# Two moves in the instruction order of a tuned fp32 kernel: GpSimd's w3 product ahead of its edge steps, ScalarE's square root one iteration later

## The chip, the cores and the metric

The kernel runs on one core of a Trainium2 chip. The metric is the device time of one execution, in microseconds, from the first to the last instruction of the program with what little lies around them. Five engines share the work: TensorE (PE in the profile; its weight loads are PEld), VectorE (DVE), ScalarE (ACT), GpSimd (POOL) and SyncE (SP), which only issues the DMAs here. Each engine runs its instructions in the order in which they were written for it. An engine that waits for a semaphore holds up all that stands behind it on its own queue.

## What is computed

Four blocks, one after the other, each add to x a chain of four style-modulated 1D convolutions over 64 samples of 64 channels and 1024 positions, in fp32:

```python
def _layer(x, style, w, b, mw, mb, typ):
    s = style @ mw.T + mb
    weight = SCALE * w * s[:, None, :, None]
    demod = lax.rsqrt(jnp.sum(weight * weight, axis=(2, 3)) + EPS)
    weight = weight * demod[:, :, None, None]
    if typ == 'same':
        out = conv_same(x, weight) + b[None, :, None]
    elif typ == 'upsample':
        out = blur(conv_up(x, weight) + b[None, :, None])
    elif typ == 'downsample':
        out = conv_down(blur(x), weight) + b[None, :, None]
    return out
# in each of four blocks, with the block's own weights:
for typ in ('same', 'upsample', 'same', 'downsample'):
    out = _layer(out, style, ...)
x = x + out
```

The weights differ from sample to sample, since the style scales them. Layers 1 to 3 of a block have nothing nonlinear between them, so for each sample the kernel folds them into one short filter.

## The kernel before

**The main loop.** It has NN = 256 iterations, one for each pair of block and sample: 4 blocks of 64 samples, the block number being k. n is the iteration, and n mod 64 the place within a block. For each sample TensorE runs `conv0` (layer 0, 6 matmuls of 512 columns, into the bank `ZP`) and `convg` (the folded filter, 12 matmuls). Every fp32 operand is held as a high and a low part, so a product is three matmuls. TensorE's iteration n issues `conv0(n + 1)`, what edge and setup work falls due, and then `convg(n)`.

**What lies between the two convolutions.** ScalarE writes the high part zh from PSUM (`zhi`, L721), VectorE then the low part zl (`zlo`, L980), and `convg` waits for zl. Ahead of `conv0` stand in the same manner xh (`xhi`, L709, ScalarE) and xl (`xlo`, L974, VectorE). After `convg` VectorE adds the result into the resident X (`xnew`, L989), and SyncE stores it.

**The folded filters.** They are made for four samples at a time (QS = 4), in a chain across the engines. GpSimd multiplies w3 by the samples' scales into w3q (`w3s`, L1279), at n = 3 mod 4. ScalarE rounds it to w3h (`w3hi`, L735) at the head of its iteration n = 0 mod 4. GpSimd makes the low parts of it (`w3lo`, L1285 and L1286). TensorE multiplies by w2 (`v_products`, output of L1010 on VectorE), then by w1 (`k_products`, weights w1h, w1l, w1d). ScalarE evicts the result to kp in eight instructions (`kev`, L750), four on either side of `zhi`, and VectorE makes the filter taps out of kp (L1031 to L1043) and their low part (L1067).

**GpSimd's iteration.** In written order it holds: in the last block `finish`, which corrects the edges of a finished sample; a gather of edge columns; `edge_apply` (L1402 to L1405); one of the four edge steps (z, y, s, o) of the block; `w3lo`; `w3s`; and tables that are built at a few iterations. The edge steps fall at n mod 64 = 4, 7, 9 and 11, in the first block at 16, 19, 21 and 23. Step y (L1369 to L1375) waits for VectorE's yq and step o (L1388) for VectorE's en. Both stand in an iteration that also has a `w3s`.

**Setup of the next block.** During a block its scales for the next one are made in stages at fixed iterations: VectorE's reciprocal and ScalarE's square root (stage RECIP) at n = 27 in the first block and at n mod 64 = 15 in the next two, VectorE's Newton step (NEWTON, L892) four iterations on. ScalarE's square root (`root`, L684) waits for VectorE's reciprocal (L883), the last work of VectorE's iteration, and stands last in ScalarE's iteration.

The functions and what calls them follow.

Of the kernel before, what the change touches and what calls it, by code (L numbers as in the profile page):

```python
# [40 lines left out]
SQUARES, STYLE, DEMOD, NEWTON, TABLES, BIAS_U, BIAS_S, SPLIT_W, SPLIT_1, RECIP = range(10)  # L41
# [47 lines left out]
def build(nc, x, ends, pack, taps, w3in, small, sets, out):  # L89
    ctx = ExitStack()  # L90
    with ctx:
# [115 lines left out]
        def where(n):  # L207

            st, i = divmod(n, GS)
            g, k = STEPS[st]  # L210
            return st, k, g * GS + i, n % (NR * GS)
# [9 lines left out]
        def v_at(n):  # L221
            if n in V_LATE or n in V_LATE.values():
                return (V_LATE[n] + V_LEAD) // QS if n in V_LATE else None
            q, i = divmod(n + V_LEAD, QS)
            return q if i == 0 and 0 <= q < NQ else None

        def g_at(n):
            if n in G_LATE or n in G_LATE.values():
                return (G_LATE[n] + G_LEAD) // QS if n in G_LATE else None
            q, i = divmod(n + G_LEAD, QS)  # L230
            return q if i == 0 and 0 <= q < NQ else None
# [27 lines left out]
        def finished_at(n):  # L259

            first = (NBLK - 1) * NB
            start = first + EDGE_SLOT + EDGE_STEPS[-1] + 1
            done, at = [], first
            for i in range(start, n + 1):
                done = list(range(at, min(at + 4, i - 1, NN)))
                at += len(done)
            return done
# [9 lines left out]
        def setup_at(n):  # L277
            k, i = n // NB + 1, n % NB
            if k == NBLK - 1 and i == LAST_BIAS_S:
                return k, (BIAS_S,)  # L280
            return (k, (SECOND_SLOTS if k == 1 else SETUP_SLOTS).get(i, ())) if k < NBLK else (None, ())
# [364 lines left out]
        def _(act):  # L646
# [4 lines left out]
            def squares(k):  # L651
                act.activation(wsq[:, 0:3], wT[:, k], ACT.Square)
                act.activation(wsq[:, 3], w1T[0:C, k], ACT.Square).then_inc(s["wsq"], 1)

            def w2hi(k):
                if k >= NW:
                    act.wait_ge(s["V"], (k - NW + 1) * NB // QS)
                act.activation(w2h[:, k % NW], w2f[:, k], ACT.Copy)
                act.activation(w2d[0:C, k % NW, 0:K], w2f[0:C, k, 0:K], ACT.Copy)
                act.activation(w2d[C:128, k % NW], w2f[0:C, k], ACT.Copy).then_inc(s["w2hi"], 1)  # L660

            def w0hi(k):
                if k >= NW:
                    act.wait_ge(s["conv0"], (k - NW + 1) * NB)
                act.activation(w0h[:, k % NW], w0f[:, k], ACT.Copy).then_inc(s["w0hi"], 1)

            def w1hi(k):
                if k >= NW:
                    act.wait_ge(s["K"], (k - NW + 1) * NB // QS)
                act.activation(w1h[0:C, k % NW, 0:K], w1T[0:C, k], ACT.Copy)  # L670
                act.activation(w1h[C:128, k % NW, 1:K + 1], w1T[C:128, k], ACT.Copy)
                act.activation(w1d[:, k % NW, 0:K], w1T[:, k], ACT.Copy).then_inc(s["w1hi"], 1)
# [9 lines left out]
            def root(l, count):  # L682
                act.wait_ge(s["rcp"], count)
                act.activation(dall[:, l, :], tmp[:, l, :], ACT.Sqrt).then_inc(s["sqrt"], 1)  # L684

            def setup(k, stage):
                if stage == SQUARES:
                    act.wait_ge(s_pack[k], 16)
                    act.wait_ge(s_taps[k], 16)
                    act.wait_ge(s["Dp"], k)  # L690
                    squares(k)
                    w2hi(k)
                    w0hi(k)
                elif stage == RECIP:
                    root(slice(0, NLAY), k + NPART)
                elif stage == SPLIT_W:
                    w1hi(k)

            def xhi(n):
                st, k, b, sl = where(n)  # L700
                act.wait_ge(s["S0"], k + 1)
                if k == 0:
                    p, use = pair_of(n)
                    act.wait_ge(s_in[p], 16 * use)
                else:
                    act.wait_ge(s["eap"], applied(st))
                if n >= 3:
                    act.wait_ge(s["conv0"], n - 2)
                act.activation(xh[n % 3][:, 0:XW], X[:, sl, :], ACT.Copy, scale=tab["S0"][:, k, b:b + 1]) \  # L709
                    .then_inc(s["xhi"], 1)  # L710
# [20 lines left out]
            def w3hi(q):  # L731
                act.wait_ge(s["w3q"], q + 1)
                if q >= 1:
                    act.wait_ge(s["V"], q)
                act.activation(w3h[:, :, :, :], w3q[:, :, :, :], ACT.Copy).then_inc(s["w3h"], 1)  # L735

            def vhi(q):
                act.wait_ge(s["vf"], q + 1)
                if q >= 1:
                    act.wait_ge(s["K"], q)  # L740
                act.activation(vh[:, 0:2, :, :], vf[:, 0:2, :, :], ACT.Copy).then_inc(s["vh"], 1)
                act.activation(vh[0:C, 2, :, :], vf[0:C, 2, :, :], ACT.Copy).then_inc(s["vh2"], 1)
# [9 lines left out]
            def kev(q, part):  # L752
                if part == 0:
                    act.wait_ge(s["K"], q + 1)
                    act.wait_ge(s["t1s"], STEPS[q * QS // GS][1] + 1)
                    act.wait_ge(s["fir"], q)
                for j in range(QS):
                    ins = evict(q, j, part)
                if part == 1:
                    ins.then_inc(s["kev"], 1)  # L760
# [82 lines left out]
            for n in range(2, NN):  # L843
                if v_at(n + 1) is not None and n + 1 not in V_LATE:
                    w3hi(v_at(n + 1))
                if n + 3 < NN:
                    xhi(n + 3)
                if g_at(n) is not None:
                    kev(g_at(n), 0)
                if n + 1 < NN:  # L850
                    zhi(n + 1)
                if g_at(n) is not None:
                    kev(g_at(n), 1)
                if g_at(n - 2) is not None:
                    ghi(g_at(n - 2))
                if v_at(n - 1) is not None:
                    vhi(v_at(n - 1))
                k, stages = setup_at(n)
                for stage in stages:
                    setup(k, stage)  # L860
                if where(n)[1] == NBLK - 1:
                    xb(n)

# [359 lines left out]
        def _(pool):  # L1223
            counts, open_ = {"w3q": 1, "w3l": 1}, {}

            def sig(ins, name="chp", by=1):

                ins.then_inc(s[name], by)
                counts[name] = open_[name] = counts.get(name, 0) + by
# [41 lines left out]
            def w3s(q):  # L1271
                st, k, b, sl = where(q * QS)
                if k >= 1:
                    pool.wait_ge(s["e2"], k)
                    pool.wait_ge(s["w3rest"], 16)
                pool.wait_ge(s["w3l"], q)
                e = tab["E2"][:, k, b:b + QS].unsqueeze(1).unsqueeze(3).broadcast_to([128, 2, QS, C])
                w = w3f[:, k, :, :].unsqueeze(2).broadcast_to([128, 2, QS, C])
                sig(pool.tensor_tensor(w3q[:, :, :, :], w, e, ALU.mult), "w3q")  # L1279
# [144 lines left out]
            pool.wait_ge(s["xlo"], 4)  # L1424
            for n in range(NN):
                st, i = divmod(n, GS)
                for m in finished_at(n):
                    finish(m)
                if i == GATHER and st >= 1 and STEPS[st - 1][1] < NBLK - 1:
                    gather(st - 1)  # L1430
                if ends_at(n) is not None:
                    ends_ready(ends_at(n))
                if i == APPLY and st + 1 < NS and STEPS[st + 1][1] >= 1:
                    edge_apply(st + 1)
                k, stage = edge_at(n)
                if k is not None:
                    (edge_z, edge_y, edge_s, edge_o)[stage](k)
                if v_at(n + 1) is not None:
                    w3lo(v_at(n + 1))
                if v_at(n + 2) is not None:  # L1440
                    w3s(v_at(n + 2))
                for k, i in build_at(n):
                    build(k, i)
                if n == FIRST_TAP_SUMS:
                    tap_sums(0)
                if n % NB == TAP_SUMS and n // NB + 1 < NBLK:
                    tap_sums(n // NB + 1)
# [70 lines left out]
```

## Time and profile before

| | |
|---|---|
| time, median of 3 runs | 1335.65 us (1335.02 to 1335.79) |
| the profiled execution's own time | 1336.1 us |
| its span, first to last instruction | 1334.3 us |
| TensorE, matmuls | busy 1301.2 us, 98% of the span |
| VectorE | busy 1150.0 us, 86% |
| ScalarE | busy 842.1 us, 63% |
| GpSimd | busy 347.3 us, 26% |
| mean granted TensorE clock | 0.991 |

A timeline row of the profile begins with its start and its length in us from the span's start. A number in brackets at its end is the time that the engine sat idle before it, with the instruction that released it. In a row of the waits stand the sum in us, how often, and the longest. A matmul's end is modelled, and in a full pipeline the next one starts before it.

### The profile page before, as it was taken

The page shows a single profiled execution, that of the slowest core. Times are in us where ns is not written, and L with a number is a line of the kernel's source. Part 1 is how long each engine was busy: PE and PEld are TensorE (multiplying, and loading weights), DVE is VectorE, ACT ScalarE, POOL GpSimd, SP SyncE. Part 2 cuts the span into 40 slices and gives each one's busy share as a digit, 9 for nine tenths or more (in the row PEclk, how much of TensorE's full clock was granted, in tenths as well). Part 3 has the DMA queues.
Part 4 walks back from the last instruction along what each step waited for, and adds up shares of the span by engine and source line. Part 5 has one row for each costly group of instructions (what it writes and reads, how often), then busy time and mean ns, then how long its engine had stood idle before and what let it go on. Part 6 is the DMA issues. An engine that isn't in the chain of part 4 may idle for free.

```text
span 1334.3 us, 20141 instructions
## 1 busy us (share of the span) xinstructions
PE 1301.2 (98%) x6565; PEld 1077.7 (81%) x6565; DVE 1150.0 (86%) x1855; ACT 842.1 (63%) x1528; POOL 347.3 (26%) x632
## 2 busy tenths in 40 slices
PE   7799999999999999999999999999999999999998
PEld 5588878888888788888888778888888878888887
DVE  6798879998988899989889789989888788898885
ACT  5656466656564666666655566566566667877774
POOL 3214221133122221124131221121522233323221
PEclk7899999999999999999999999999999999999999
DMA  9235655546554465454556445565554257655643
GB/s 312 77 100 163 166 146 125 159 149 186 170 149 113 135 186 170 141 172 121 162 172 171 140 112 158 164 178 162 164 146 124 93 121 190 186 170 146 177 121 99
DMA packets 95368, 203.38 MB, mean 152 GB/s; under 512 B 10720, under 2 KB 12256, under 8 KB 95264
## 3 DMA queue, kind: packets, MB, share of 16 engines
q1 hardware_dynamic: 94896, 201.81, 52.7%
q8 instruction: 54, 0.88, 0.3%
q14 instruction: 50, 0.41, 0.1%
q10 hardware_dynamic: 368, 0.28, 0.1%
HBM read 72.39 MB, written 67.24 MB: 105 GB/s over the span
## 4 chain that ended last, share of the span: by engine, by line
PE 75%; DVE 15%; ACT 4%; issue 3%; POOL 2%; DMA 1%; SPq 0%; ACTq 0%; DVEq 0%; POOLq 0%
PE ps L463 74%; ACT kp L750 2%; DVE gl L1067 2%; DVE gf L1031 2%; DVE zl L980 2%; DVE xl L974 2%; DVE X L989 1%; DVE vf L1010 1%; DVE gf L1037 1%; ACT xh L709 1%; DVE vl L1017 1%; DVE vh L1019 1%; POOL w3q L1279 1%; DVE v L1015 0%; DVE gf L1043 0%
## 5 line engine op out<-in xcount | busy, mean ns | idle before, releaser
L463 PE MATMUL ps<-zh,gh 128*128 128x512 f32 (+1 forms) x1028 | 411.1, 400 | 16.2 <-DVE zl L980 12.2
L463 PE MATMUL ps<-zl,gh 128*128 128x512 f32 (+1 forms) x1028 | 407.5, 396 | 0.0
L721 ACT ACTIVATE zh<-ps,t_bx 128x512 fp32r<-128x512 f32 x256 | 175.7, 686 | 271.4 <-PE ps L463 267.9
L463 PE MATMUL ps<-zh,gl 128*128 128x512 f32 (+1 forms) x1028 | 283.0, 396 | 0.0
L750 ACT ACTIVATE kp<-ps,t_T1s 64x256 f32<-64x256 f32 x512 | 213.5, 465 | 102.8 <-PE ps L463 99.5
L463 PEld LDWEIGHTS ps<-zh,gh 128*128 128x128 f32 x1028 | 195.0, 190 | 70.0 <-DVE zl L980 20.7
L989 DVE SCALAR_TENSOR_TENSOR X<-ps,t_D,X 128x512 f32<-128x512 f32 x255 | 190.0, 745 | 61.9 <-PE ps L463 35.4
L974 DVE SCALAR_TENSOR_TENSOR xl<-X,t_S,xh 128x513 fp32r<-128x513 f32 x256 | 202.1, 809 | 35.0 <-ACT xh L709 32.8
L980 DVE SCALAR_TENSOR_TENSOR zl<-ps,t_bx,zh 128x512 fp32r<-128x512 f32 x256 | 190.7, 745 | 48.1 <-ACT zh L721 45.2
L463 PEld LDWEIGHTS ps<-zl,gh 128*128 128x128 f32 x1028 | 195.4, 190 | 44.6
L463 PEld LDWEIGHTS ps<-zh,gl 128*128 128x128 f32 x1028 | 194.7, 189 | 45.4
L1285 POOL TENSOR_TENSOR w3h<-w3q,w3h 64x256 fp32r<-64x256 f32 x63 | 59.6, 946 | 537.5 <-ACT w3h L735 535.5
L709 ACT ACTIVATE xh<-X,t_S 128x513 fp32r<-128x513 f32 x256 | 183.7, 718 | 1.2
L463 PE MATMUL ps<-xh,w0l 128*128 128x512 f32 x512 | 161.7, 397 | 2.7 <-POOL w0l L1269 2.7
L463 PE MATMUL ps<-xh,w0h 128*128 128x512 f32 x512 | 161.2, 396 | 1.4 <-ACT xh L709 1.4
L463 PE MATMUL ps<-xl,w0h 128*128 128x512 f32 x512 | 160.9, 395 | 0.2 <-DVE xl L974 0.2
L1031 DVE SCALAR_TENSOR_TENSOR gf<-kp,gf 128x384 f32<-128x384 f32 (+1 forms) x260 | 148.6, 572 | 6.8
L1067 DVE TENSOR_TENSOR gl<-gf,gh 64x896 fp32r<-64x896 f32 x126 | 138.6, 1100 | 2.0
L770 ACT ACTIVATE gh<-gf 64x896 fp32r<-64x896 f32 x126 | 120.2, 954 | 3.6
L463 PEld LDWEIGHTS ps<-xh,w0l 128*128 128x128 f32 x512 | 96.5, 189 | 26.3 <-POOL w0l L1269 3.1
L463 PEld LDWEIGHTS ps<-xl,w0h 128*128 128x128 f32 x512 | 96.5, 189 | 23.9 <-DVE xl L974 0.6
L463 PEld LDWEIGHTS ps<-xh,w0h 128*128 128x128 f32 x512 | 87.3, 188 | 12.8 <-ACT xh L709 1.6
(204 smaller groups left out, 1541.3 us busy)
## 6 DMA issues: line engine op xcount, KB each, us to landing
out_x<-X SPq DMA_DIRECT2D x255, 256.5 KB, 4.9
X<-out_x SPq DMA_DIRECT2D x96, 513.0 KB, 7.0
gh<-gh SPq DMA_DIRECT2D x127, 240.0 KB, 3.0
gl<-gl SPq DMA_DIRECT2D x127, 240.0 KB, 3.6
X<-x_in SPq DMA_DIRECT2D x32, 513.0 KB, 7.6
pk<-taps_in SPq DMA_DIRECT2D x3, 512.0 KB, 12.0
pk<-pack_in SPq DMA_DIRECT2D x3, 352.0 KB, 11.2
pk<-sets_in SPq DMA_DIRECT2D x4, 256.0 KB, 8.4
```

Of the source, the lines that this page charges most:

```text
L463: return pe.matmul(out_ap, a, b, start=first, stop=last, skip_group_check=True)
L709: act.activation(xh[n % 3][:, 0:XW], X[:, sl, :], ACT.Copy, scale=tab["S0"][:, k, b:b + 1]) \
L721: act.activation(zh[n % 2][:, ZPAD:ZPAD + M], ps[:, ZP + n % 2, :], IDENT, bias=tab["bx"][:, k, b:b + 1]).then_inc(s["zhi"], 1)
L750: return act.activation(kp[rows, to, i, :], got[of, :, j, :], ACT.Copy, scale=tab["T1s"][of, k, b:b + 1])
L770: act.activation(dst, gf[rows], ACT.Copy).then_inc(s["gsh"], 1)
L974: dve.scalar_tensor_tensor(xl[n % 3][:, 0:XW], X[:, sl, :], tab["S0"][:, k, b:b + 1], xh[n % 3][:, 0:XW].bitcast(F32), ALU.mult, ALU.subtr ...
L980: dve.scalar_tensor_tensor(zl[n % 2][:, ZPAD:ZPAD + M], ps[:, ZP + n % 2, :], tab["bx"][:, k, b:b + 1], zh[n % 2][:, ZPAD:ZPAD + M].bitcas ...
L989: dve.scalar_tensor_tensor(X[:, sl, 0:M], ps[:, OP + n % 2, :], tab["D3"][:, k, b:b + 1], X[:, sl, 0:M], ALU.mult, ALU.add).then_inc(s["xn ...
L1010: dve.tensor_tensor(vf[:, :, :, :], pv, e, ALU.mult).then_inc(s["vf"], 1)
L1031: return dve.scalar_tensor_tensor(dve_out, kp[rows, of, i, :], factor, dve_out, ALU.mult, ALU.add)
L1067: dve.tensor_tensor(dst, gf[rows], own(gh, h)[1].bitcast(F32), ALU.subtract).then_inc(s["gsl"], 1)
L1285: link(pool.tensor_tensor(w3h[C:128, 1], w3q[C:128, 1], hi[C:128, 1], ALU.subtract))
```

## The change

On GpSimd the call of `w3s` goes from behind the edge step and `w3lo` to the head of the iteration, ahead of `finish`, the gather, `edge_apply` and the edge step. On ScalarE the stage RECIP, which is only the square root there, is run one iteration later than its slot, at the end of that iteration. VectorE's reciprocal and Newton step stay where they were. No instruction is added or taken away.

```diff
@@ scalar, for n in range(2, NN) @@
                 if v_at(n - 1) is not None:
                     vhi(v_at(n - 1))
+                k, stages = setup_at(n - 1)
+                if RECIP in stages:
+                    setup(k, RECIP)
                 k, stages = setup_at(n)
                 for stage in stages:
-                    setup(k, stage)
+                    if stage != RECIP:
+                        setup(k, stage)
                 if where(n)[1] == NBLK - 1:
                     xb(n)
@@ gpsimd, for n in range(NN) @@
                 st, i = divmod(n, GS)
+                if v_at(n + 2) is not None:
+                    w3s(v_at(n + 2))
                 for m in finished_at(n):
                     finish(m)
...
                     (edge_z, edge_y, edge_s, edge_o)[stage](k)
                 if v_at(n + 1) is not None:
                     w3lo(v_at(n + 1))
-                if v_at(n + 2) is not None:
-                    w3s(v_at(n + 2))
                 for k, i in build_at(n):
                     build(k, i)
```

GpSimd's order at edge steps z and y of the second block (n = 68 to 72), before the change: ze is step z, ye is step y, w3q is the product.

```order
L1361 TENSOR_TENSOR ze<-ze,t_T 128x192
L1285 TENSOR_TENSOR w3h<-w3q,w3h 64x256
L1286 TENSOR_TENSOR w3l<-w3q,w3h 128x256
L1369 TENSOR_TENSOR ye<-yq,t_ub 128x192
L1370 TENSOR_TENSOR ye<-yq,t_ub 64x2x64
L1371 TENSOR_TENSOR ye<-yq,t_ub 64x64
L1372 TENSOR_TENSOR ye<-yq,t_ub 64x2x64
L1373 TENSOR_TENSOR ye<-yq,t_ub 64x64
L1375 TENSOR_TENSOR ye<-ye 64x64
L1279 TENSOR_TENSOR w3q<-w3f,t_E 128x512
L1285 TENSOR_TENSOR w3h<-w3q,w3h 64x256
```

The same place on GpSimd after the change, where all line numbers from here on are four higher:

```order
L1365 TENSOR_TENSOR ze<-ze,t_T 128x192
L1289 TENSOR_TENSOR w3h<-w3q,w3h 64x256
L1290 TENSOR_TENSOR w3l<-w3q,w3h 128x256
L1283 TENSOR_TENSOR w3q<-w3f,t_E 128x512
L1373 TENSOR_TENSOR ye<-yq,t_ub 128x192
L1374 TENSOR_TENSOR ye<-yq,t_ub 64x2x64
L1375 TENSOR_TENSOR ye<-yq,t_ub 64x64
L1376 TENSOR_TENSOR ye<-yq,t_ub 64x2x64
L1377 TENSOR_TENSOR ye<-yq,t_ub 64x64
L1379 TENSOR_TENSOR ye<-ye 64x64
L1289 TENSOR_TENSOR w3h<-w3q,w3h 64x256
```

The product has moved over the six instructions of step y, to right behind the low parts of the product before it.

ScalarE's order around the second block's square root (scr is the setup's scratch, L684 the root), before the change:

```order
L709 ACTIVATE xh<-X,t_S 128x513
L721 ACTIVATE zh<-ps,t_bx 128x512
L684 ACTIVATE scr<-scr 128x256
L735 ACTIVATE w3h<-w3q 128x512
L709 ACTIVATE xh<-X,t_S 128x513
L750 ACTIVATE kp<-ps,t_T1s 64x4x64 x4
L721 ACTIVATE zh<-ps,t_bx 128x512
L750 ACTIVATE kp<-ps,t_T1s 64x4x64 x4
L709 ACTIVATE xh<-X,t_S 128x513
```

And after it:

```order
L709 ACTIVATE xh<-X,t_S 128x513
L721 ACTIVATE zh<-ps,t_bx 128x512
L735 ACTIVATE w3h<-w3q 128x512
L709 ACTIVATE xh<-X,t_S 128x513
L750 ACTIVATE kp<-ps,t_T1s 64x4x64 x4
L721 ACTIVATE zh<-ps,t_bx 128x512
L750 ACTIVATE kp<-ps,t_T1s 64x4x64 x4
L684 ACTIVATE scr<-scr 128x256
L709 ACTIVATE xh<-X,t_S 128x513
```

The root has moved behind one whole iteration of a group's first sample, with its eight evictions. The orders of TensorE, VectorE and SyncE are the same as before.

## Rows read from the trace of the kernel before

**Rows 1.** The page: busy us, share of the span and instructions by engine.

```profile
PE 1301.2 (98%) x6565; PEld 1077.7 (81%) x6565; DVE 1150.0 (86%) x1855; ACT 842.1 (63%) x1528; POOL 347.3 (26%) x632
```

**Rows 2.** Who waited for whom: us in total, times, longest us.

```profile
ACT w3h L735 <- POOL w3q L1279: 59.0, 10, 8.4
...
DVE zl L980 <- ACT zh L721: 45.2, 50, 2.7
...
ACT scr L684 <- DVE scr L883: 16.1, 3, 5.4
...
PE ps L463 <- DVE zl L980: 12.2, 15, 2.2
```

**Rows 3.** Timeline of PE: two waits in the first block.

```profile
194.12 0.50 PE L463 MATMUL ps<-zh,gh 128*128 128x512 f32 x1 [1.34 <-DVE zl L980]
...
309.42 0.49 PE L463 MATMUL ps<-zh,gh 128*128 128x512 f32 x1 [0.44 <-DVE zl L980]
```

**Rows 4.** Timeline of PE: the waits in the second block.

```profile
415.88 0.50 PE L463 MATMUL ps<-zh,gh 128*128 128x512 f32 x1 [0.33 <-DVE zl L980]
...
437.86 0.50 PE L463 MATMUL ps<-zh,gh 128*128 128x512 f32 x1 [0.80 <-DVE zl L980]
...
459.06 0.50 PE L463 MATMUL ps<-zh,gh 128*128 128x512 f32 x1 [1.29 <-DVE zl L980]
...
475.08 0.50 PE L463 MATMUL ps<-zh,gh 128*128 128x512 f32 x1 [0.34 <-DVE zl L980]
```

**Rows 5.** Timeline of PE: the waits in the last block.

```profile
1062.52 0.50 PE L463 MATMUL ps<-zh,gh 128*128 128x512 f32 x1 [0.58 <-DVE zl L980]
...
1072.60 0.50 PE L463 MATMUL ps<-zh,gh 128*128 128x512 f32 x1 [0.24 <-DVE zl L980]
...
1085.99 0.56 PE L463 MATMUL ps<-zh,gh 128*128 128x512 f32 x1 [2.21 <-DVE zl L980]
```

**Rows 6.** Windows of two convg: start:end length, busy, PEclk, DMA share, GB/s.

```profile
1079.36:1082.21 2.85, 2.85 (x13) 1.00 0.00 0
1085.99:1090.44 4.45, 4.45 (x13) 0.62 0.97 186
```

**Rows 7.** Timeline of POOL around step y of the second block.

```profile
392.74 0.74 POOL L1286 TENSOR_TENSOR w3l<-w3q,w3h 128x256 fp32r<-128x256 f32 x1
407.48 0.60 POOL L1369 TENSOR_TENSOR ye<-yq,t_ub 128x192 f32<-128x192 f32 x1 [14.01 <-DVE yq L1095]
...
410.45 1.04 POOL L1279 TENSOR_TENSOR w3q<-w3f,t_E 128x512 f32<-128x512 f32 x1
```

**Rows 8.** Timeline of ACT at the same place.

```profile
402.68 0.67 ACT L721 ACTIVATE zh<-ps,t_bx 128x512 fp32r<-128x512 f32 x1
411.52 0.64 ACT L735 ACTIVATE w3h<-w3q 128x512 fp32r<-128x512 f32 x1 [8.18 <-POOL w3q L1279]
...
414.35 0.69 ACT L721 ACTIVATE zh<-ps,t_bx 128x512 fp32r<-128x512 f32 x1
```

**Rows 9.** Timeline of DVE at the same place.

```profile
412.81 0.75 DVE L974 SCALAR_TENSOR_TENSOR xl<-X,t_S,xh 128x513 fp32r<-128x513 f32 x1 [2.79 <-ACT xh L709]
...
415.07 0.75 DVE L980 SCALAR_TENSOR_TENSOR zl<-ps,t_bx,zh 128x512 fp32r<-128x512 f32 x1 [0.85 <-ACT zh L721]
```

**Rows 10.** Timeline of PE at the same place: the last k_products matmul.

```profile
408.60 0.28 PE L463 MATMUL ps<-vh,w1d 128*128 128x256 f32 x1
```

**Rows 11.** Timelines of POOL and ACT ahead of step o, second block.

```profile
424.57 0.23 POOL L1405 TENSOR_SCALAR X<-Bk 64x8 f32<-64x8 f32 x1
...
433.50 0.63 ACT L735 ACTIVATE w3h<-w3q 128x512 fp32r<-128x512 f32 x1 [6.07 <-POOL w3q L1279]
```

**Rows 12.** Timelines of DVE and ACT at the second block's root.

```profile
452.62 1.74 DVE L883 RECIPROCAL scr<-scr 128x256 f32<-128x256 f32 x1
...
454.39 0.42 ACT L684 ACTIVATE scr<-scr 128x256 f32<-128x256 f32 x1 [5.36 <-DVE scr L883]
```

**Rows 13.** Timeline of DVE: one form alone, and beside a product on POOL.

```profile
374.57 0.56 DVE L1031 SCALAR_TENSOR_TENSOR gf<-kp,gf 128x384 f32<-128x384 f32 x1
...
376.17 1.32 DVE L1031 SCALAR_TENSOR_TENSOR gf<-kp,gf 128x384 f32<-128x384 f32 x1
```

## The prediction

> **What bounds the kernel now.** I read the page's busy shares first. TensorE is busy 98% of the span, VectorE 86%, ScalarE 63%, GpSimd 26% [rows 1]. So only time that TensorE loses can be won, and an idle GpSimd or ScalarE is worth nothing by itself. The list of waits comes next. After the start-up TensorE waits for one thing, VectorE's low part zl: 12.2 us in 15 waits. VectorE in its turn waits for ScalarE's zh, and ScalarE has two long waits of its own: 59.0 us in ten for GpSimd's product w3q, and 16.1 us in three for VectorE's reciprocal [rows 2]. The third view is TensorE's timeline, to see where the 15 waits stand.
>
> In the second block there are four. The first two, 0.33 and 0.80 us, come one iteration after a late w3q (steps y and o). The third, 1.29 us, comes behind the root, the fourth, 0.34 us, at the Newton step [rows 4]. The third block repeats these within 0.05 us each. The first block has the root's 1.34 us, and 0.44 us at n = 52, where neither part of the change does anything [rows 3]. The last block has no setup: 0.58, 0.24 and 2.21 us, all around its steps y to o [rows 5]. What is left of the 12.2, 12.2 - 2 x 2.76 - 1.78 - 3.03 = 1.87 us, belongs to steps y and o of the first block.
>
> **Why these are waits for ScalarE.** At step y of the second block GpSimd is done with the earlier low parts at 392.74 + 0.74 = 393.48. It then stands 14.01 us before step y, for VectorE's yq, and starts the product only at 410.45 [rows 7]. ScalarE is ready for the product at 411.52 - 8.18 = 403.34, and waits to 411.52. Its next zh starts at 414.35 [rows 8]. VectorE sits idle 2.79 us for the xh of the same iteration and 0.85 us for that zh [rows 9], and TensorE idles until zl is there.
>
> **Part one, w3s first.** It moves over step y or step o at eight places, two in each block, and in the last block over `finish` as well. With it at the head of n = 71 the product can start at 393.48, end a microsecond later, and be there 8.8 us before ScalarE asks at 403.34. At step o the work ahead of it (`edge_apply`) ends at 424.57 + 0.23 = 424.80, so the product ends at about 425.9, and ScalarE asks at 433.50 - 6.07 = 427.43 [rows 11]. That is 1.5 us early, the smaller of the two margins.
>
> What is the next thing late? Without the wait ScalarE makes w3h and xh and is then held by TensorE's k_products, whose last matmul ends at 408.88 [rows 10]. Between the start of w3h at 411.52 and zh at 414.35 lie w3h and xh, some 1.1 us, and four evictions, 1.7 us [rows 8]. So zh would start near 410.6 instead of 414.35, 3.7 us sooner. VectorE is free at 412.81 - 2.79 = 410.02; xl and xnew take it to 411.5, and zl behind them, whose zh ends at 411.3, to 412.3 [rows 9]. TensorE wants zl at 415.88 - 0.33 - 0.16 = 415.4 [rows 4]. So nothing else is late there, with 3 us in hand, and the whole wait goes. Step y itself is not delayed: GpSimd is idle for 13 us between the moved product and step y.
>
> The nine product places: 1.87 + 2 x 1.13 + 3.03 = 7.16 us. I count the 0.24 us among them, since it stands two iterations behind a late product with VectorE still catching up.
>
> **Part two, the root.** It leaves a place where ScalarE stands 5.36 us for a reciprocal that runs from 452.62 to 454.36 [rows 12], and in its new place, some 6 us on, the reciprocal is long done. It costs there its own 0.42 us, ahead of the xh for three samples on. The Newton step, the only reader, comes three iterations behind the new place, about 15 us. The gain is 1.34 + 2 x 1.29 = 3.92 us.
>
> **Two things that the idle times leave out.** A matmul that waits starts later than a pipelined one by more than its idle time. 12 matmuls take 2.85 us, so they start 0.24 us apart [rows 6], while one is shown as 0.40 us long. That is 0.16 us for each of the 12 waits: 1.9 us. And behind the wait of 2.21 us the granted clock is 0.62 over the convg, against 1.00 for a usual one; that is the low level of 1.2 GHz for most of it, and the convg takes 4.45 instead of 2.85 us [rows 6]. TensorE had been idle 2.21 us before the clock fell. Without the wait I expect no fall: 1.60 us.
>
> **The sum.** 7.16 + 3.92 + 1.9 + 1.60 = 14.6 us. It is made on the profiled execution, 1336.1 us with a span of 1334.3; the median is 1335.65, and I take the difference off that: **1321.0 us**. The two waits at the Newton steps (0.34 us each, 0.5 with the overlap) may go too, as VectorE reaches them without the backlog of the root's wait. That is up to 1.0 us more, which I leave to the range. The 0.44 us at n = 52 stays.
>
> **A cost that the trace shows: VectorE beside GpSimd.** The same VectorE instruction takes 0.56 us alone and 1.32 us when it starts with a product on GpSimd beside it, 0.76 us more [rows 13]. Before, the late products ran while VectorE waited anyway: 410.45 lies in its idle time before 412.81 [rows 7, 9]. Moved, they run beside VectorE's work, as all the other products do. The bounds are 0 and 0.76 us for each of eight. I take 0 for TensorE. The ordinary products pay this in VectorE's slack, with no wait of TensorE behind them, and VectorE has 14% of its time idle.
>
> The Trainium skill (SBUF — State Buffer, "Who interferes with whom") says that a VectorE instruction with two SBUF inputs and a GpSimd instruction that reads SBUF exclude each other for a whole instruction. By this rule, the trace agrees: the extra 0.76 us is most of a product's 1.04 us. It speaks against the move, and gives the third case below.
>
> **The rivals.**
> - **All waits go, as above.** 1321.0 us, and 1319.5 to 1323.5 with the Newton waits gone or one or two of the others kept. For it: every one of the 12 waits stands behind a long wait of ScalarE, and where a product is on time TensorE waits for zl only at n = 52 and at Newton steps. Chance 0.68.
> - **VectorE takes over as the late one.** Between n = 71 and n = 84 it has extra work (steps y, s and o, reciprocal, Newton), and TensorE's waits gave it time. If half of the 12 waits came back as waits for a zl that is late by itself, the gain would be 7.3 us: 1328.3 us. Against it: the idle 2.79 and 0.85 us in that very iteration. Chance 0.16.
> - **VectorE is shut out by the moved products, on the path.** Each of the eight costs at most a product, 1.04 us: 14.6 - 8.3 = 6.3 us gain, 1329.4 us. It would need VectorE without slack at n = 68 to 75, and TensorE's timeline shows no wait there. Chance 0.06.
> - **Nothing measurable.** The waits of ScalarE were beside the path, or the product is still held at the head of the iteration (it waits for the low parts of the one before, done at 393.48). Then 1335 us. Chance 0.05.
> - **Slower: the lock, with nothing won.** One mechanism again, VectorE's lost time. If TensorE's waits were set by VectorE's own work and not by ScalarE, nothing is won at them. The eight moved products then add 0.76 us each: 1335.65 + 6.1 = 1341.7 us. It decides from the point where VectorE has no idle time ahead of zl; it has 3.6 us at the place that I read. Chance 0.05.
>
> In the last block `finish` comes 1.04 us later in a few iterations, and with it a store, which a later load of the same slot waits for. That happens once for a sample and doesn't add up, so I give it no case.
>
> **How the numbers follow.** Faster holds the first three cases, 0.90; same 0.05; slower 0.05. No change is within 0.2%, 2.7 us, about what a measurement of this kernel tells from none. The range leaves out the two last cases and half of the third: 1319.0 to 1328.5 us.
>
> **What the new profile would show.** ScalarE's waits for w3q fall from ten and 59.0 us to one or two, about 5 us in all; its waits for the reciprocal are gone; TensorE's waits for zl fall from 12.2 to between 0.4 and 1.2 us; no low clock behind n = 204; GpSimd's step y still starts behind a wait for yq. I am wrong if zl is still late after n = 72 or 80 with ScalarE's zh long done, or if VectorE's busy time grows by several microseconds and shows again on TensorE.

## The result, and the profile after

The changed kernel takes 1318.25 us, the median of four runs (1316.51 to 1319.12), against 1335.70 us for the kernel before beside it (1335.02 to 1335.79). The ratio is 0.9869, with a 95% interval of 0.9852 to 0.9886: 17.45 us less. The forecast was 1321.0 us, with a range of 1319.0 to 1328.5. The sign and the mechanism were right; the median lies 0.75 us below the range's lower end.

The profiled execution took 1317.87 us, its span is 1316.0 us. The page of the changed kernel, busy time by engine, answers to [rows 1]:

```profile
PE 1294.8 (98%) x6565; PEld 1077.2 (82%) x6565; DVE 1155.7 (88%) x1855; ACT 840.8 (64%) x1528; POOL 353.5 (27%) x632
```

The instruction counts are the same. VectorE's busy time grew by 5.7 us and GpSimd's by 6.2 us, for the same work; two more profiles of the changed kernel have VectorE busy 1154.1 and 1154.0 us. The list of waits, against [rows 2]:

```profile
DVE zl L984 <- ACT zh L721: 45.6, 47, 2.2
...
ACT w3h L735 <- POOL w3q L1283: 4.1, 2, 2.9
...
ACT scr L684 <- DVE scr L887: 0.6, 1, 0.6
...
PE ps L463 <- DVE zl L984: 0.4, 1, 0.4
```

ScalarE's waits for the product went from 59.0 us to 4.1, those for the reciprocal from 16.1 to 0.6 (that one is in the start-up), and TensorE's for zl from 12.2 us in 15 to 0.4 in one. VectorE's own wait for zh stayed at 45 us. It is the largest row of the four and was worth nothing, since TensorE did not stand behind it.

Step y of the second block on GpSimd, against [rows 7]:

```profile
388.13 0.74 POOL L1290 TENSOR_TENSOR w3l<-w3q,w3h 128x256 fp32r<-128x256 f32 x1
389.04 1.28 POOL L1283 TENSOR_TENSOR w3q<-w3f,t_E 128x512 f32<-128x512 f32 x1 [0.17 <-POOL w3l L1290]
403.72 0.60 POOL L1373 TENSOR_TENSOR ye<-yq,t_ub 128x192 f32<-128x192 f32 x1 [13.40 <-DVE yq L1099]
```

The product starts as soon as the low parts before it are done, and step y still stands 13.40 us for yq: it isn't delayed. ScalarE there, against [rows 8]:

```profile
399.41 0.62 ACT L735 ACTIVATE w3h<-w3q 128x512 fp32r<-128x512 f32 x1
399.93 0.72 ACT L709 ACTIVATE xh<-X,t_S 128x513 fp32r<-128x513 f32 x1
404.33 1.67 ACT L750 ACTIVATE kp<-ps,t_T1s 64x256 f32<-64x256 f32 x4 [3.69 <-PE ps L463]
406.02 0.69 ACT L721 ACTIVATE zh<-ps,t_bx 128x512 fp32r<-128x512 f32 x1
```

The wait of 8.18 us is gone, and what holds ScalarE is TensorE's k_products, as the prediction said. A wait for the engine that is to be kept busy costs nothing. VectorE, against [rows 9]:

```profile
406.04 0.74 DVE L978 SCALAR_TENSOR_TENSOR xl<-X,t_S,xh 128x513 fp32r<-128x513 f32 x1
406.70 0.74 DVE L993 SCALAR_TENSOR_TENSOR X<-ps,t_D,X 128x512 f32<-128x512 f32 x1
407.37 0.73 DVE L984 SCALAR_TENSOR_TENSOR zl<-ps,t_bx,zh 128x512 fp32r<-128x512 f32 x1
```

Its idle 2.79 and 0.85 us are gone, and zl ends at 408.10. TensorE starts the convg that reads it at 410.76, without a wait, and the window of the convg that follows n = 204 is at full clock, against 4.45 us and 0.62 in [rows 6]. The two rows are from the timeline of TensorE and from the windows (start:end length, busy, PEclk, DMA share, GB/s):

```profile
410.76 0.48 PE L463 MATMUL ps<-zh,gh 128*128 128x512 f32 x1
```
```profile
1069.63:1072.48 2.85, 2.85 (x14) 1.00 0.95 175
```

**Where the 18.3 us between the two spans are.** TensorE's order is the same in both kernels, so the start of each convg can be subtracted from the start of the same one before. This difference grows in steps:

| place | convg (n) | forecast, us | measured, us |
|---|---|---|---|
| products, steps y and o | 21, 25, 73, 77, 137, 141, 201, 203, 205 | 7.16 + 9 x 0.16 = 8.60 | 8.82 |
| root | 29, 81, 145 | 3.92 + 3 x 0.16 = 4.40 | 4.43 |
| clock in the convg at n = 205 | to 206 | 1.60 | 1.66 |
| Newton step | 32, 84, 148 | 0, left to the range | 1.20 |
| slow first matmuls (below) | some 16 | 0 | 1.6 |
| start-up, before n = 5 | | 0 | 0.46 |
| tail | | 0 | 0.16 |
| sum | | 14.6 | 18.3 |

Of the 1.66 us of the clock's row, 0.13 are those of a slow first matmul. On the row of the slow first matmuls: the first matmul after a wait for zl is shown as 0.50 us long and the second starts 0.33 us behind it, instead of 0.40 and 0.23. These are two convg of the kernel before, the first in the full pipeline; the first row of the other stands in [rows 4], and its second is the last row here:

```profile
410.13 0.40 PE L463 MATMUL ps<-zh,gh 128*128 128x512 f32 x1
410.36 0.39 PE L463 MATMUL ps<-zl,gh 128*128 128x512 f32 x1
...
416.21 0.39 PE L463 MATMUL ps<-zl,gh 128*128 128x512 f32 x1
```

This is 0.10 us a wait, and gone wherever a wait went, except at n = 73, 137 and 201 (and mostly 21), where the first matmul stays slow in the changed kernel too (0.48 us in the row of 410.76 above); matmuls of another shape stand ahead of the convg there. The same 0.10 us also stood in the kernel before at n = 32, 85, 149, 202 and 216, where TensorE shows no idle time and zl ends just 0.05 or 0.06 us ahead of the convg. So it goes with a zl that is only just there, and not only with a wait. From n = 16 to the last convg the kernel took 1205.82 us before and 1188.12 after, 17.70 less. The 0.46 us of start-up are in a part that the change hardly touches: in the thirteen profiles of this study the convg of n = 16 starts anywhere between 121.6 and 123.3 us. I count them as scatter.

### The profile page after: what moved, and what is told of

Read it like the earlier page. It is cut to its first block, busy times and chain, and to the rows that moved or that the text cites. A ratio compares the mean times of both kernels' runs of the same rounds, so it can differ in the third digit from the quotient of the medians.

```text
span 1316.0 us, 20135 instructions
## 1 busy us (share of the span) xinstructions
PE 1294.8 (98%) x6565; PEld 1077.2 (82%) x6565; DVE 1155.7 (88%) x1855; ACT 840.8 (64%) x1528; POOL 353.5 (27%) x632
## 4 chain that ended last, share of the span: by engine, by line
PE 95%; DVE 3%; issue 1%; ACT 1%; POOL 0%; DMA 0%; SPq 0%; ACTq 0%; DVEq 0%; POOLq 0%
PE ps L463 93%; PE ps L565 1%; PE ps L395 1%; DVE gf L1035 0%; PE ps L443 0%; DVE gl L1071 0%; DMA gh<-gh 0%; DVE xl L978 0%; DVE vf L1014 0%; DVE vl L1021 0%; DVE gf L1041 0%; DVE vh L1023 0%; DVE zl L984 0%; ACT kp L750 0%; DVE X L993 0%
## 5 line engine op out<-in xcount | busy, mean ns | idle before, releaser
L1035 DVE SCALAR_TENSOR_TENSOR gf<-kp,gf 128x384 f32<-128x384 f32 (+1 forms) x260 | 153.5, 590 | 6.8
```

The costliest lines, as they stand in the source:

```text
L1035: return dve.scalar_tensor_tensor(dve_out, kp[rows, of, i, :], factor, dve_out, ALU.mult, ALU.add)
```

## The experiments

The first two kernels do one part each. Beside each set of runs the kernel before was timed on the same chip: 1336.17 us for e1 to e4, 1335.64 for f1 to f4, 1335.74 for g1 to g3.

**e1_product_only: the product moved, the root in its old place.**

```diff
@@ scalar, against the changed kernel @@
-                k, stages = setup_at(n - 1)
-                if RECIP in stages:
-                    setup(k, RECIP)
                 k, stages = setup_at(n)
                 for stage in stages:
-                    if stage != RECIP:
-                        setup(k, stage)
+                    setup(k, stage)
```

> The changed kernel with ScalarE's root back in its old place; only GpSimd's w3 product is moved. Main theory: the two parts add up, and the three waits at the root (1.3 us each, about 1.5 us with the overlap) and the waits at the Newton steps behind them (0.2 and 2 x 0.5 us) belong to the root alone. Then this kernel wins 18.3 - 4.4 - 1.2 - 0.4 = 12.3 us in the profiled span, about 1323.5 us, and its TensorE timeline shows waits for zl at the three roots and at the Newton steps of the second and third block. Rival: the Newton waits are VectorE's backlog from steps y, s and o behind the late products. Then they are gone here too and this kernel stands at about 1322.3 us with only the root's waits and the one at n = 52.

Measured: 1321.78 us (ratio 0.9892, 0.9879 to 0.9906), a gain of 14.4 us, more than either expectation had. TensorE's timeline of this kernel, at the roots of the first and the second block and at the second Newton step:

```profile
190.93 0.50 PE L463 MATMUL ps<-zh,gh 128*128 128x512 f32 x1 [0.23 <-DVE zl L980]
...
453.15 0.50 PE L463 MATMUL ps<-zh,gh 128*128 128x512 f32 x1 [0.21 <-DVE zl L980]
...
469.19 0.49 PE L463 MATMUL ps<-zh,gh 128*128 128x512 f32 x1 [0.36 <-DVE zl L980]
```

The root's waits are 0.2 us, not 1.3, though the root was not moved [rows 3, 4]. ScalarE still stands for the reciprocal, but 4.8 us each instead of 5.4. The Newton waits are still there.

**e2_root_only: the root moved, the product in its old place.**

```diff
@@ gpsimd, against the changed kernel @@
                 st, i = divmod(n, GS)
-                if v_at(n + 2) is not None:
-                    w3s(v_at(n + 2))
                 for m in finished_at(n):
...
                     w3lo(v_at(n + 1))
+                if v_at(n + 2) is not None:
+                    w3s(v_at(n + 2))
```

> The kernel before with only ScalarE's root moved one iteration later; GpSimd's order is the old one. Main theory: three root waits (4.4 us), their slower first matmuls (0.3 us) and the Newton waits (1.2 us) go, 5.9 us: about 1329.8 us. The nine waits behind the late products stay with the low clock behind n = 204. Rival (Newton waits come from the products): 4.7 us, about 1331.0 us, and the timeline still shows TensorE waiting 0.34 us at n = 84 and 148.

Measured: 1330.92 us (ratio 0.996, 0.9948 to 0.9973), a gain of 5.25 us. The time is the rival's (1331.0), but the waits are those of the main theory: the root's waits are gone, the Newton waits too, and those of the products all stay. Some 0.27 us a block comes back one iteration ahead of the old place, at n = 28, 80 and 144, where zl is now only just there. Newton's 1.2 us therefore belong to the root: they are there in e1, and in neither kernel in which the root is moved.

The two gains add to 14.4 + 5.25 = 19.6 us, against the 17.45 of both. By the intervals of the ratios each of the three is uncertain by about 2 us, so the medians alone don't show that the parts overlap. The starts do: from n = 16 to the last convg e1 gains 14.38 us, e2 5.33 and both together 17.70, so that **the parts overlap by 2.0 us** in the profiled executions, and by 2.7 without a wait at n = 212 that has another cause (f3 below). With the product moved alone three quarters of the root's waits are gone already: 0.39 us a block in the starts, against 1.48 before, together 3 x 1.1 = 3.3 us. Of this the three places of 0.27 us take back 0.8.

The wait of 2.2 us at n = 205 is here too, but not the low clock. The timeline of TensorE and the window of that convg in this kernel:

```profile
1080.38 0.50 PE L463 MATMUL ps<-zh,gh 128*128 128x512 f32 x1 [2.22 <-DVE zl L984]
```
```profile
1080.38:1083.23 2.85, 2.85 (x12) 1.00 0.99 160
```

TensorE goes on at 1.00 and catches up with VectorE, which is still late: zl ends 0.05 us ahead of the convg of n = 206, against 1.58 us in the kernel before. What follows costs 1.2 us by n = 209, most of it ahead of the convg of n = 208:

```profile
1094.43 0.74 PE L463 MATMUL ps<-vl,w1h 128*128 128x256 f32 x4 [0.38 <-DVE vl L1021]
```

In the kernel before, the slow convg gives VectorE this time. From the start of n = 205 to that of n = 209 the kernel before takes only 0.33 us longer than e2, although its one convg is 1.53 us slower. Another 0.70 us is lost in e2 at n = 212, for the cause shown at f3.

**e3_late_at_203: of the changed kernel's products one is late again, the one of n = 203, behind step o.**

```diff
-                if v_at(n + 2) is not None:
+                if v_at(n + 2) is not None and n != 203:
                     w3s(v_at(n + 2))
...
                     w3lo(v_at(n + 1))
+                if v_at(n + 2) is not None and n == 203:
+                    w3s(v_at(n + 2))
```

> The changed kernel, but at the one iteration n = 203 the product stays behind step o. It measures the disputed price of that one wait. Main theory: a wait of TensorE of about 2.2 us at n = 205, and the granted clock at its low level over the convg behind it: 2.4 + 1.7 = 4.1 us more than the changed kernel, about 1322.3 us. Rival: the low clock before was set by what went ahead of it (waits at n = 201 and 203 too), which are gone here. Then the clock stays at 1.00 and it is 2.4 us, about 1320.7 us.

Measured: 1321.17 us (ratio 0.9889, 0.9874 to 0.9904), 2.9 us over the changed kernel's 1318.25 (2.7 by the ratios, and 2.7 by the starts of the two profiles). That is near the rival's 2.4, but the wait of 2.2 us at n = 205 that both expectations had isn't there. Two rows of its waits, and two of TensorE's timeline:

```profile
ACT w3h L735 <- POOL w3q L1283: 8.7, 3, 4.2
...
PE ps L463 <- DVE zl L984: 1.0, 2, 0.6
```
```profile
1080.13 0.50 PE L463 MATMUL ps<-zh,gh 128*128 128x512 f32 x1 [0.56 <-DVE zl L984]
...
1107.34 0.47 PE L463 MATMUL ps<-zh,gh 128*128 128x512 f32 x1 [0.62 <-issue]
```

ScalarE stands 4.2 us for the one late product, and yet TensorE starts n = 205 without a wait, by 0.06 us. The cost comes later, in steps of 0.82, 0.76 and 0.78 us at n = 207, 208 and 212, and the clock stays at 1.00. The last of these is not the product's (f3 below), so the late product costs 1.9 us by n = 209. It makes no wait of 2.2 us at n = 205 as in the kernel before, presumably because there VectorE still carries the lag of the late product of step y: at n = 203 zl is 0.06 us ahead in the kernel before and 2.52 in e3. No run has just these two products late. A product that is late by itself is paid one or more convg on.

**e4_second_product: the changed kernel, with a second, equal product into a spare tile behind each one from the second block on (48 more).**

```diff
                 sig(pool.tensor_tensor(w3q[:, :, :, :], w, e, ALU.mult), "w3q")
+                if NB <= 4 * q:
+                    link(pool.tensor_tensor(dum[:, :, :, :], w, e, ALU.mult))
```

> The changed kernel, and from the second block on GpSimd makes each product a second time, into a scratch tile that nobody reads, right behind the first: 48 more instructions of 1.04 us that read what w3s reads. It doubles the suspected cost of products beside VectorE's work. Main theory: VectorE loses up to 0.4 to 0.8 us at each, 20 to 35 us of busy time in all, and has the slack for it, so TensorE gets at most one or two short waits: within 2 us of the changed kernel, about 1319 us. Rival: VectorE is close to being the bound. Then half or more of the loss returns as waits for zl, 10 us or more: over 1328 us.

Measured: 1327.31 us (ratio 0.9928, 0.9916 to 0.9941), 9.1 us slower than the changed kernel (7.9 by the ratios); the spans differ by 9.5. The page, TensorE's longest wait, and the one at n = 116:

```profile
PE 1300.5 (98%) x6565; PEld 1077.8 (81%) x6565; DVE 1181.5 (89%) x1855; ACT 840.7 (63%) x1528; POOL 414.0 (31%) x680
```
```profile
473.71 0.51 PE L464 MATMUL ps<-zh,gh 128*128 128x512 f32 x1 [0.85 <-DVE zl L985]
...
627.77 0.50 PE L464 MATMUL ps<-zh,gh 128*128 128x512 f32 x1 [0.42 <-DVE zl L985]
```

VectorE, which got no work, is busy 25.8 us longer, 0.54 us for each added product, and a third of that, 8.4 us between n = 16 and the last convg, returns on TensorE (0.7 of it at n = 212, see f3). My expectation of at most 2 us fell. VectorE's idle 12% is not free where it counts. In the changed kernel zl ends 1.41 us ahead of its convg at n = 80, but only 0.46, 0.34 and 0.44 us ahead at n = 84, 85 and 88, around the Newton step. The margin is smallest at n = 116 and 180, 0.05 us, at the place in the second and third block where the wait of n = 52 stands in the first. Waits now stand at 84 and 85, at 116 and 180, and in small amounts at other places.

**f1_late_at_75_root_old: e1 with one product late again, that of n = 75, behind step o of the second block.** It asks whether a late product four iterations ahead is what makes the root's wait long.

```diff
@@ gpsimd, against e1_product_only @@
-                if v_at(n + 2) is not None:
+                if v_at(n + 2) is not None and n != 75:
                     w3s(v_at(n + 2))
...
+                if v_at(n + 2) is not None and n == 75:
+                    w3s(v_at(n + 2))
```

> The changed kernel with the root in its old place, and with one product, that of n = 75 (second block, step o), left behind its edge step. It asks why the root's waits were 1.5 us in the kernel before and only 0.4 us with the products moved. Carried lag: a late product leaves VectorE 1.1 us behind, and nothing before the root lets it catch up. Then TensorE waits at n = 77 (0.2 us or less from a single late product), and at the second block's root, n = 81, the whole 1.5 us are back, while the third block's root, n = 145, with all its products on time, stays at 0.4 us. Rival: each wait is its own, and the smaller root waits come from something else in the order; then n = 81 and n = 145 show the same 0.4 us.

Measured: 1322.03 us (ratio 0.9901, 0.9884 to 0.9917). The roots of the second block (n = 81, product late) and of the third (n = 145, product on time), in one execution:

```profile
452.53 0.50 PE L463 MATMUL ps<-zh,gh 128*128 128x512 f32 x1 [0.88 <-DVE zl L980]
...
773.09 0.50 PE L463 MATMUL ps<-zh,gh 128*128 128x512 f32 x1 [0.21 <-DVE zl L980]
```

The late product makes no wait at n = 77, where it would be looked for, and adds 0.67 us of idle time at the root, four convg later. VectorE carried the lag there: against e1, zl is ahead of its convg by 1.87 instead of 2.53 us at n = 79 and by 1.12 instead of 1.78 at n = 80, 0.66 us less both times. In the kernel before, 1.46 and 0.71 us, it is 1.07 us less, which is the whole difference between its root's wait of 1.29 us and e1's 0.21. Of the 1.5 us in steps that I expected, f1 has 1.04, against 0.38 with the product on time. The product of step y, on time here, presumably had the rest; no run has it late alone.

**f2_before_again and f3_after_again: both kernels once more, for the clock and for the scatter.**

> The kernel before once more, for a second profile of it. If the wait of 2.2 us at n = 205 brings the low clock with it, the granted clock over the convg behind it is about 0.6 again and that convg takes 4.4 us. If the low clock there is chance, as the root-only kernel's profile makes likely (same wait, clock 1.00), it may be missing here, and then small waits for zl at n = 207 to 212 take its place, with the same span within 1 us.

> The changed kernel once more, on the same chip and beside the same runs of before as the kernels of this call. Earlier 1318.25 us, ratio 0.987. Expected the same ratio within its interval, 1317 to 1320 us, with the waits of TensorE gone but for n = 52.

The kernel before took 1335.67 us, with all 15 waits again and the low clock too: 2.23 us idle at n = 205, and then

```profile
1085.63:1090.08 4.45, 4.45 (x13) 0.63 0.94 162
```

The changed kernel took 1318.15 us (ratio 0.9868, 0.9853 to 0.9883). Its profile has a wait of 0.57 us at n = 212 that the first profile of the same kernel hasn't, and a third profile (g3 below) has one of 0.75 us. The profile names no releaser for it:

```profile
1105.78 0.48 PE L463 MATMUL ps<-zh,gh 128*128 128x512 f32 x1 [0.75 <-issue]
```

The program does. At the first sample of a group TensorE also waits for a DMA by SyncE that copies the high parts of a pair of filters from one half of the partitions to the other (`ghd`). Its issue, in the first profile and in g3, and behind it the rows of the DMA view with its size and its time to landing in us, in the same order:

```profile
1097.65 0.47 SPq L344 DMA_DIRECT2D gh<-gh  x1
...
1097.88 0.66 SPq L344 DMA_DIRECT2D gh<-gh  x1
```
```profile
gh<-gh SPq DMA_DIRECT2D x1, 240.0 KB, 5.7
...
gh<-gh SPq DMA_DIRECT2D x1, 240.0 KB, 7.8
```

In all thirteen profiles the copy is issued 1.03 us ahead of the convg of n = 211, and it takes 5.7 to 7.8 us to land. Where it takes 7.5 us or more (f3, g3, e2, e3 and e4), TensorE waits, and starts 0.09 us after the landing. GpSimd, which stands for another load at that time (6.89 us in the first profile, 8.02 in g3), isn't the cause: its product there starts 2.35 us behind the convg of n = 211 in the first profile, without the wait, and 2.41 us behind it in g3, with it.

**f4_split1_at_45: the changed kernel, with the stage SPLIT_1 of the next block's setup two iterations earlier, against the last wait for zl, at n = 52.**

```diff
-SECOND_SLOTS = {..., 43: (SPLIT_W,), 47: (BIAS_U, SPLIT_1)}
+SECOND_SLOTS = {..., 43: (SPLIT_W,), 45: (SPLIT_1,), 47: (BIAS_U,)}
```

> The changed kernel, with VectorE's low parts of w1 (the stage ahead of GpSimd's table building) two iterations earlier in the first block. In the profile the building waits 2.4 us for them at n = 48 and then falls beside VectorE's tap instructions, which take twice their time; TensorE's last wait for zl follows at n = 52. If that is its cause, the wait of 0.45 us (0.6 with the overlap, and 0.2 at n = 51) is gone in the profile, about 0.8 us less than the changed kernel, little more than the timing can tell. Rival: VectorE's extra work only moves, and a wait for zl stands at another iteration from 46 to 53.

Measured: 1317.71 us (ratio 0.9864, 0.9849 to 0.9879). The first row is the changed kernel at n = 52, the second this one there:

```profile
304.83 0.49 PE L463 MATMUL ps<-zh,gh 128*128 128x512 f32 x1 [0.45 <-DVE zl L984]
```
```profile
303.43 0.50 PE L463 MATMUL ps<-zh,gh 128*128 128x512 f32 x1
```

The wait is down to 0.11 us, below what the row shows, and the start is 0.65 us sooner by the step; but 0.65 us is less than the times can tell: the changed kernel beside it (f3) took 1318.15 us.

**g1_product_two_earlier: the product another two iterations earlier from the second group on, against the wait at n = 212. g2_both: g1 and f4 together. g3_after_beside: the changed kernel beside them.**

```diff
-                if v_at(n + 2) is not None:
-                    w3s(v_at(n + 2))
+                ahead = n + 2 if n < GS else n + 4
+                if v_at(ahead) is not None:
+                    w3s(v_at(ahead))
```

> The changed kernel with the w3 product two iterations earlier still (at the head of n = 1 mod 4, from n = 9 on). That puts it ahead of the edge correction at n = 2 mod 8, on which GpSimd stands 7 to 8 us in the last block until a load has landed (n = 210); the product of n = 211 is behind it. Theory: that late product is what is left of the cause, and it shows as a wait of TensorE of 0.7 us at n = 212 in some executions and not in others. Then ScalarE waits for w3q only at the start, no profile shows a wait at n = 212, and the median falls by 0.2 to 0.7 us against the changed kernel, at the edge of what can be told. Rival: the earlier product changes nothing on TensorE's timeline, or its overlap with VectorE brings a new wait for zl; then the same or up to 1 us more.

> The product two iterations earlier, and the low parts of w1 two iterations earlier in the first block (the edit that took 0.65 us from the wait at n = 52). If the two are independent, 0.8 to 1.3 us under the changed kernel beside it: about 1317 us, ratio to before 0.986. If not, the median lies within 0.5 us of the changed kernel.

> The changed kernel beside the two others of this call, as their yardstick: 1317 to 1320 us, ratio 0.987. In its profile a wait at n = 212 of 0.6 us or none.

Measured: g1 1319.19 us (0.9874, 0.9859 to 0.9889), g2 1318.35 us (0.987, 0.9854 to 0.9887), g3 1318.11 us (0.9868, 0.9853 to 0.9883). Both expected gains failed: g1 is 1.1 us above g3 and g2 0.2, within the intervals. The wait at n = 212, 0.75 us in g3's profile, is absent in g1, but not by the edit: the copy is issued at the same place and took 6.8 us, so that it landed 0.16 us ahead of the convg. The theory that the late product makes this wait was wrong. g1 is also 0.5 us slower around n = 52, and a new wait stands near the start of the loop:

```profile
83.53 0.49 PE L463 MATMUL ps<-zh,gh 128*128 128x512 f32 x1 [0.31 <-DVE zl L984]
```

None of the three versions can be told from the changed kernel by its time, so I found none that beats it.

## Why the prediction was right in kind and too small in size

**What bounds the kernel: right.** TensorE is busy 98% in both; all that was won is time that it had lost.

**Part one: right, and well sized.** All waits behind late products are gone at once, 8.82 us against 8.60. The product of step y ends 9.1 us before ScalarE starts on it (390.32 against 399.41), nothing else became late (the next thing was k_products, as said), and step y wasn't delayed.

**Part two: right, and well sized for the root itself,** 4.43 us against 4.40. The sum gave it these as its own, though. They are its own only with the late products beside it; with the product on time the root's waits were 0.2 us each (e1), and f1 shows the lag being carried there. For the change as a whole this made no difference, since both parts were made; for either part alone the additive sum would mislead.

**Newton waits left at zero: the first step that failed.** I had seen that they could go when VectorE no longer carries the root's backlog, priced them at up to 1.0 us, and took 0. They went, 1.20 us, and e1 against e2 shows that it was the root's doing: with the root in its old place VectorE carries its lag to them (in e1 zl is 1.17 us ahead at n = 82, in the changed kernel 2.10). The forecast of the likeliest case should have had them.

**"A matmul that waits starts later than a pipelined one by more than its idle time": right, but sized at 0.16 us where it is 0.26; the second step that failed.** The 0.16 came from the ends of the matmul ahead of a wait. The rows on which I worked show the waiting matmul as 0.50 us long [rows 3 to 5], and the next one starts 0.10 us late because of it. In all, 1.6 us, with the places that have no idle time. This was in the rows, and I read past it. The two terms, 1.20 and 1.6 us, are most of the 3.7 us by which the span fell more than the sum. The rest is 0.46 us of start-up, 0.16 of tail and some 0.3 in the other rows.

**The clock, 1.60 us: right in sum, not in cause.** 1.66 us came back. But e2 had the same wait of 2.22 us and kept 1.00, while the kernel before fell to 0.62 and 0.63 in two executions. So the wait is not enough to make the clock fall, and what decides is open. It also isn't a cost on top: without the low clock e2 pays 1.2 us by n = 209 for VectorE's lag, so that the low clock cost only 0.33 us more than the same wait without it. Most of the 1.66 us was the lag's price in another form, and went because the lag did. That the sum came out is luck.

**Contention taken as 0: right for this change, for a weaker reason than I gave.** VectorE's busy time is 4.0 to 6.0 us longer in three profiles of the changed kernel than in two of the kernel before. That is 0.5 to 0.75 us for each of eight moved products, if it is all theirs; e2, which moves the root alone, has 2.2 us of it too. The bound was 0.76. One row shows the loss, of VectorE beside the product that starts at 389.04:

```profile
389.34 1.12 DVE L1043 SCALAR_TENSOR_TENSOR gf<-kp 128x128 f32<-128x128 f32 x1
```

This form's mean over its 63 instructions is 0.37 us. The product itself took 1.28 us instead of 1.04 [rows 7]. The Trainium skill (SBUF — State Buffer, "Who interferes with whom") has the later of two such instructions blocked until the other is done. The trace agrees roughly: 1.12 us from 389.34 ends at 390.46, and the product ends at 390.32, but the 0.14 us between are less than the 0.28 us that the form takes at its shortest. No wait of TensorE followed. Yet e4 shows that "VectorE's slack" was no ground for it in general: near n = 84 to 88 that slack is under half a microsecond, and at n = 116 and 180 it is 0.05 us. The moved products were free because of where they run. That of step y runs during the convg of n = 69, and the zl after it, for n = 70, is ahead by 1.26 us instead of 2.09. The rows are zl and the convg, before and after:

```profile
395.20 0.74 DVE L980 SCALAR_TENSOR_TENSOR zl<-ps,t_bx,zh 128x512 fp32r<-128x512 f32 x1
...
398.03 0.40 PE L463 MATMUL ps<-zh,gh 128*128 128x512 f32 x1
```
```profile
391.44 0.75 DVE L984 SCALAR_TENSOR_TENSOR zl<-ps,t_bx,zh 128x512 fp32r<-128x512 f32 x1
...
393.44 0.40 PE L463 MATMUL ps<-zh,gh 128*128 128x512 f32 x1
```

So VectorE's margin there is 0.83 us smaller, a little more than the bound of 0.76, and 1.26 us was left. Two convg earlier, at n = 68, only 0.43 us would have been there to take. At n = 73 and 77, where the waits had stood, zl is ahead by 2.66 and 2.25 us.

**The rivals.** "VectorE takes over" and "shut out, on the path" didn't happen at this size; e4 shows both on the way, with 48 more products. "Slower" was far off: the waits at the products and at the root were not set by VectorE's own work, since they went when ScalarE's did.

**The range.** Its lower end, 1319.0, lies 2.0 us under the forecast: 1.0 us for the Newton waits, and 1.0 us for nothing that was named. Scatter had no term. The runs of the changed kernel alone go from 1316.5 to 1319.2 us, and those of the kernel before, over all sets, from 1334.5 to 1337.0. Part of this is seen: the wait at n = 212, for the copy of the filters, is 0, 0.57 or 0.75 us in three profiles of one kernel. Profiled and median times differ too, by 0.4 us up in the kernel before and 0.4 down in the changed one, which is why 18.3 us of span are 17.45 in the medians.

## What to carry to other kernels

Price a wait by the starts of the instruction that waits and of the one behind it, beside the same pair in a full pipeline, and not by the idle time: here a wait cost its idle time and 0.26 us, or 0.18 behind matmuls of another shape. A late input is often paid some iterations on, on an engine that carries the lag; before adding up the gains of two edits, ask whether they clear the same lag. An engine's idle share over the span says nothing of its margin: list how early its result is at each place where it is waited for, and take the smallest. Where the profile names no releaser for a wait, look in the program for what the instruction waits for, and compare the DMA's landing in several executions before naming a cause.

## What was not expected of the hardware

- The granted clock fell to 0.62 and 0.63 behind an idle time of 2.2 us of TensorE in two executions of the kernel before, and stayed at 1.00 behind one of 2.22 us at the same place in e2. What made the difference isn't settled by these runs.
- The first 128x512 matmul behind an idle time is 0.50 us long against 0.40, and the first behind matmuls of another shape is 0.48 us with no idle time shown (410.76).
- VectorE's busy time grew by 0.54 us for each GpSimd product of 1.04 us that was added (e4: 25.8 us for 48), with no work added on VectorE.
- The same DMA copy of 240 KB, issued at the same place, took between 5.7 and 7.8 us to land in thirteen profiles, and a wait of TensorE for it comes and goes with that.
